# Router logits of eight batches by one product each, zero rows stored one block later, first queries and keys loaded ahead of the raw weights

## The reference

```python
xn = _layernorm(x)                                   # layer 0
s = attn0(xn)                                        # rms norm, queries, keys, values, running sums
router_logits = silu(xn @ router_w1) @ router_w2     # [8, 512, 16]
expert_probs = softmax(router_logits.transpose(0, 2, 1), axis=-1)   # over the 512 tokens
expert_weights, token_indices = top_k(expert_probs, 64)             # per sequence and expert
# gather these tokens, run the expert on them, add the weighted rows onto zeros
g = silu(output); x = x + s * g
xn = _layernorm(x)                                   # layer 1
s = attn1(layernorm(xn) * ln_scale + ln_bias) + ...  # 16 heads, softmax(q k / 16) v
g = silu(ffn1(xn))                                   # 8 experts, 2 per token, and one shared expert
x = x + s * g
```

## Time and profile before

| | us |
|---|---|
| median of 3 runs | 1772.76 (1771.67 to 1774.93) |
| the profiled execution, its own time | 1770.29 |
| its span, first to last instruction | 1768.3 |
| PE busy | 1576.7 (89%) |
| DVE busy | 1166.1 (66%) |
| ACT busy | 918.9 (52%) |
| POOL busy | 739.4 (42%) |
| granted TensorE clock over the span | 0.942 of full |

### The profile page before, as it was taken

One profiled execution on the slowest core, in us unless ns is written; L12 is line 12 of the kernel. 1 busy time (PEld: TensorE's weight loads), 2 busy tenths in 40 slices (PEclk: granted clock), 3 DMA queues, 4 the chain that ended last, 5 costly groups with the idle time before them and its releaser, 6 DMA issues.

```text
span 1768.3 us, 27041 instructions
## 1 busy us (share of the span) xinstructions
PE 1576.7 (89%) x9562; PEld 1140.3 (64%) x9562; DVE 1166.1 (66%) x1847; ACT 918.9 (52%) x1426; POOL 739.4 (42%) x664
## 2 busy tenths in 40 slices
PE   6679999999999549954999999999999999999976
PEld 4357767877877435632677777777777777777631
DVE  6747567567557156656766666777777777777647
ACT  2335545545545123311555556777776777676644
POOL 3406335334433255502323223556565555555410
PEclk9899999999999869975999999999999999999975
DMA  6715546445333268845233335767676667666464
GB/s 223 232 37 114 149 96 141 122 99 141 74 90 87 24 214 293 308 161 150 87 107 114 100 124 137 196 159 195 165 188 161 182 165 185 175 176 184 115 187 147
DMA packets 218918, 265.38 MB, mean 150 GB/s; under 512 B 19616, under 2 KB 160416, under 8 KB 218784
## 3 DMA queue, kind: packets, MB, share of 16 engines
q1 hardware_dynamic: 191904, 227.92, 42.6%
q0 software_dynamic: 26880, 35.73, 11.3%
HBM read 174.30 MB, written 88.75 MB: 149 GB/s over the span
## 4 chain that ended last, share of the span: by engine, by line
PE 39%; SPq 4%; DVE 3%; DMA 2%; ACT 1%; issue 1%; POOL 0%; DVEq 0%; ACTq 0%
PE a_hidden_bank L93 16%; PE a_bank L93 8%; PE a_bank L1522 5%; PE a_max_bank L1491 5%; PE a_score_bank L1512 3%; DMA a_ka<-qk 2%; SPq L1314 2%; SPq L1318 2%; PE a_max_bank L1537 1%; PE a_bank L1529 1%; DVE a_w20lo L1828 1%; ACT a_xThi L1670 1%; DVE a_neg_max L1787 1%; DVE a_hT1lo L1818 0%; SPq L1380 0%
## 5 line engine op out<-in xcount | busy, mean ns | idle before, releaser
L1648 ACT ACTIVATE a_prob<-a_score_bank 128x1024 f32<-128x1024 f32 x240 | 246.2, 1026 | 257.1 <-PE a_score_bank L1512 214.9
L1787 DVE TENSOR_REDUCE a_neg_max<-a_max_bank 128x2 f32<-128x1024 f32 x249 | 304.1, 1221 | 91.8 <-PE a_max_bank L1491 86.2
L1444 POOL DMA_INDIRECT fs<-a_y,a_token x80 | 127.1, 1589 | 189.2 <-ACT a_y L1696 164.9
L1491 PE MATMUL a_max_bank<-a_ka,a_qa 48*128 48x512 f32 x498 | 128.0, 511 | 23.4 <-DVE a_neg_max L1787 12.0
L1522 PE MATMUL a_bank<-a_prob,a_va 128*32 128x512 f32 x1024 | 147.2, 650 | 0.5 <-DVE a_ml L1796 0.5
L602 POOL DMA_INDIRECT f<-e_ye,c_slot_row x64 | 100.7, 1573 | 84.6 <-issue 64.6
L1810 DVE SCALAR_TENSOR_TENSOR a_tg<-a_tg,a_hidden_bank 128x512 f32<-128x512 f32 x112 | 76.7, 685 | 82.1 <-ACT a_tg L1658 82.1
L1512 PE MATMUL a_score_bank<-a_qa,a_ka 50*128 50x512 f32 x480 | 100.2, 413 | 5.1 <-DMA a_qa<-a_ml 2.7
L702 DVE TENSOR_TENSOR e_h<-e_bank,e_sge 128x512 f32<-128x512 f32 x64 | 44.3, 691 | 89.2 <-ACT e_sge L508 82.6
L358 PE MATMUL e_bank<-m_wqkv,x_rows 128*128 128x512 f32 (+1 forms) x256 | 91.3, 501 | 8.8 <-DVE e_qkv L642 8.8
L1491 PEld LDWEIGHTS a_max_bank<-a_ka,a_qa 48*128 48x128 f32 x498 | 47.9, 189 | 69.9 <-DVE a_neg_max L1787 23.3
(11 more groups left out here) (352 smaller groups left out, 4782.0 us busy)
## 6 DMA issues: line engine op xcount, KB each, us to landing
a_raw<-in_W SPq DMA_DIRECT2D x120, 512.0 KB
e_raw<-in_w SPq DMA_DIRECT2D x48, 512.0 KB, 3.8
a_qa<-qk SPq DMA_DIRECT2D x192, 64.0 KB
a_ka<-qk SPq DMA_DIRECT2D x192, 64.0 KB
xs<-c_pad SPq DMA_DIRECT2D x20, 516.0 KB
a_xg<-xs SPq DMA_DIRECT2D x20, 516.0 KB, 4.7
qk<-p_hi SPq DMA_DIRECT2D x32, 256.0 KB, 5.8
qk<-p_lo SPq DMA_DIRECT2D x32, 256.0 KB, 5.4
```

Source lines behind the costliest of these rows:

```text
L1444: nc.gpsimd.indirect_dma_start(f_rows, bass.IndirectOffsetOnAxis(token[x % 4][:, t:t + 1], 0), y[:, t, :], None, compute_op=ALU.add).then_ ...
L1491: nc.tensor.matmul(max_bank(g, m)[:, s, :], qa[q][rows, p, t * P:(t + 1) * P], ka[q][rows, p, :], start=True, stop=True).then_inc(p1_ps, 1)
L1648: nc.scalar.activation(prob[j % 2][:, 2 * p:2 * p + 2, :], score_bank(g, u)[:], ACT.Exp, scale=float(D) ** -0.5).then_inc(p_done, 1)
L1787: nc.vector.tensor_reduce(neg_max[:, g % 2, :, T * p + t], max_bank(g, m)[:], AX.X, ALU.max, negate=True).then_inc(mx_done, 1)
```

## The change

- `layer0_norm`, SP: `x[2]` and `x[3]` are loaded behind `rw2`, and later ones four turns ahead instead of two. `wqkv` and `wout` are loaded after the store of turn 3. The eight stores of zeros leave this block. The load of `rw2` waits for POOL's new fill.
- `layer0_norm`, PE, ACT and DVE: `rw2` lies in the middle of a tile of 240 columns of zeros. For turn n a window of 128 columns is taken, such that the 16 experts come to stand at rows 16n to 16n+15 of one PSUM bank, and the eight turns are accumulated in it: one product of 128 by 512 a turn in place of four of 128 by 16. ACT copies the bank once at the end; DVE's eight copies go. The result has (sequence, expert) on the partitions already.
- `layer0_norm`, POOL: fills the tile with zeros, and the six instructions for `m.r2`, `m.r2sq` and `m.r2neg` run in each turn over 4 columns, between one turn's `rstd` and the next.
- `layer0_mix_and_experts`: PE's four transposes of the logits are gone; the maximum and the exponential read `k.logits` in SBUF. SP stores the eight tiles of zeros behind the loads of the first expert's weights.
- `layer1_attend_and_feed`: SP issues `load_qk(0)` ahead of the two `load_w`; ACT does `high_x(0)` ahead of the two `high_w`.

```diff
@@ layer0_norm, SP
             sp.dma_start(rw1[:], w["rw1"]).then_inc(r_in, 16)
-            sp.dma_start(rw2[:], w["rw2"]).then_inc(r_in, 16)
-            sp.dma_start(m.wqkv[:], w["wqkv"]).then_inc(m.w_in, 16)
+            sp.wait_ge(half_set, 2)
+            sp.dma_start(rw2[:, P - E0:P], w["rw2"]).then_inc(r_in, 16)
+            load_x(2)
+            load_x(3)
             for n in range(NB):
-                if n + 2 < NB:
-                    load_x(n + 2)
+                if n + 4 < NB:
+                    load_x(n + 4)
                 sp.wait_ge(xn_done, n + 1)
                 sp.dma_start(at(xn_b, n), xn[n % 2][:]).then_inc(xn_out[n % 2], 16)
-            sp.dma_start(m.wout[:], w["wout"]).then_inc(m.w_in, 16)
-            for c in range(NB):
-                sp.dma_start(at(f_b, c), k.pad[:, :, 0:D]).then_inc(m.zeroed, 16)
+                if n == 3:
+                    sp.dma_start(m.wqkv[:], w["wqkv"]).then_inc(m.w_in, 16)
+                    sp.dma_start(m.wout[:], w["wout"]).then_inc(m.w_in, 16)
@@ PE
-                if n >= 2:
-                    pe.wait_ge(lg_sb, n - 1)
-                for t in range(T):
-                    ins = nc.tensor.matmul(B[6 + n % 2][:, t * E0:(t + 1) * E0], hT[:, n % 2, t * P:(t + 1) * P], rw2[:], start=True, stop=True)
-                ins.then_inc(lg_ps, 1)
+                first = (NB - 1 - n) * E0
+                nc.tensor.matmul(B[6][:], rw2[:, first:first + P], hT[:, n % 2, :], start=n == 0, stop=n == NB - 1).then_inc(lg_ps, 1)
@@ ACT, behind its loop
+            act.wait_ge(lg_ps, NB)
+            nc.scalar.activation(k.logits[:], B[6][:], ACT.Copy).then_inc(lg_sb, 1)
+            act.wait_ge(lg_sb, 1)
@@ POOL
+            first.step(nc.gpsimd.memset(m.half[:], -0.5))
+            first.step(nc.gpsimd.memset(rw2[:], 0.0))
             for n in range(NB):
+                now = slice(n * T, (n + 1) * T)
                 pool.wait_ge(veps_done, n + 1)
                 nc.gpsimd.tensor_tensor(rstd[:, n, :], veps[:, n, :], m.half[:, 0:T], ALU.pow).then_inc(rstd_done, 1)
-            pool.wait_ge(rstd_done, NB)
-            ... (six instructions over all 32 columns)
+                pool.wait_ge(rstd_done, n + 1)
+                own.step(nc.gpsimd.tensor_tensor(small[:, 0, now], flat_rstd[:, now], flat_rstd[:, now], ALU.mult))
+                own.wait()
+                ... (the same six instructions over the turn's 4 columns)
+                own.step(nc.gpsimd.tensor_tensor(m.r2[:, now], small[:, 2, now], m.half[:, now], ALU.pow))
@@ DVE
-                if n >= 3:
-                    logits(n - 3)
-            for n in range(NB - 3, NB):
-                logits(n)
-            dve.wait_ge(lg_sb, NB)
@@ layer0_mix_and_experts, SP
                 load(i, 0)
+            for c in range(NB):
+                sp.dma_start(at(f_b, c), k.pad[:, :, 0:D]).then_inc(m.zeroed, 16)
@@ PE
-            for t in range(T):
-                ins = nc.tensor.transpose(GATE[:, t * P:(t + 1) * P], k.logits[:, t].rearrange("p b e -> p (b e)"), k.ident[:])
-            ins.then_inc(choice_ps, 1)
@@ ACT and DVE
-            nc.scalar.activation(ex, GATE[:], ACT.Exp, bias=neg_max[:], accum_out=total[:]).then_inc(choice_exp, 1)
+            nc.scalar.activation(ex, k.logits[:], ACT.Exp, bias=neg_max[:], accum_out=total[:]).then_inc(choice_exp, 1)
-            dve.wait_ge(choice_ps, 1)
-            nc.vector.tensor_reduce(neg_max[:], GATE[:], AX.X, ALU.max, negate=True).then_inc(choice_done, 1)
+            nc.vector.tensor_reduce(neg_max[:], k.logits[:], AX.X, ALU.max, negate=True).then_inc(choice_done, 1)
@@ layer1_attend_and_feed, SP
             load_x(0)
+            load_qk(0)
             load_w(0, 0)
             load_w(1, 0)
-            load_qk(0)
             load_qk(1)
@@ ACT
+            high_x(0)
             high_w(0, 0)
             high_w(1, 0)
-            high_x(0)
```

53 lines of the change are left out of this document (24 added, 29 removed).

## The result

The change made the kernel faster, by more than forecast: 1760.72 us median (1758.33 to 1762.83, 4 runs) beside 1772.22 (1771.08 to 1774.93, 4 runs) of the kernel before on the same chip. The ratio is 0.9933, with a 95% interval of 0.9915 to 0.995. I had forecast 1766.4, with a range of 1763.0 to 1772.0: the gain is 11.5 us, not 6.4. The profiled execution of after took 1758.33 us, with a span of 1756.6.

What follows compares the result with a forecast made beforehand. A chain of waits, not engine load, was taken to bound the two changed stretches, and PE the rest. Gains of 1.6 + 0.4 + 4.4 = 6.4 us take the median from 1772.8 to 1766.4 us, range 1763.0 to 1772.0.

Steps and rivals of the forecast that it cites:

- Norm block, 1.6 forecast: layer0_norm: earlier loads and the new logits path end the block at 49.9 instead of 51.48, 1.6 us gained.
- POOL for the pacemaker: layer0_norm: with the factors in every turn, POOL takes 4.0 us a turn, longer than PE and ACT's 3.65, and sets the pace.
- the ring: layer0_norm: PE and ACT's cycle of hidden, silu and copies, 3.65 us a turn; alone it puts the last hidden at 45.1.
- rival of a contended power: layer0_norm: DVE's work slows POOL's powers, 4.4 us a turn, 2.8 us lost; total 1769.2 us, chance 0.12.
- rival of a far slower POOL: layer0_norm: semaphore hand-overs beside DVE make POOL's turn 5.5 us, costing 10.5; total 1776.9 us, chance 0.10.
- Experts' start, 0.4 forecast: Start of the experts' block: without the transposes the exponential waits only for its table load, 0.4 us gained, bounds 0 and 0.7.
- Attention block, 4.4 forecast: Start of the attention block: keys and low_x both come earlier, so DVE's first maximum does, 4.4 us gained (2.7 to 4.4).
- the landing: Attention block's start: turn 0's keys land 4.01 us after their issue ends, as in the loop, at 812.3.
- rival of early keys: Attention block's start: keys land before 811.9, low_x is last, 1 to 1.6 us more gained; 1765.1 us, chance 0.10.
- the loop: Last block's loop: PE's own work sets its pace, so its length stays unchanged and the 4.4 us gained ahead remain.
- late keys: Attention block's start: keys land as late after their issue as before (5.7 us), 1.7 less gained; 1768.1 us, chance 0.10.
- eaten gain: Shifted blocks: PE's clock steps down elsewhere or late weights catch the loop, two to five us given back; 1771 us, chance 0.12.

Runs made afterwards that it cites:

- e2: The changed kernel, unchanged, run and traced a second time: 1760.40 us, ratio 0.9934 to the kernel before.
- e7: The changed kernel with POOL's six factor instructions behind its loop again, over all 32 columns at once: 1762.65 us, ratio 0.9952 to before.
- e11: The kernel before with only the new load order of x, wqkv and wout in layer0_norm: 1768.40 us, ratio 0.9985 to before.
- e12: The changed kernel with only layer0_norm's load order of x, wqkv and wout put back: 1762.48 us, ratio 0.9956 to before.
- e8: The changed kernel with the eight stores of zeros back at the end of the norm block: 1761.81 us, ratio 0.9946 to before.
- e3: The kernel before with only the two reorderings (SP's and ACT's) at the attention block's start: 1767.56 us, ratio 0.9973 to before.
- e1: The kernel before, unchanged, run and traced a second time: 1769.63 us, 2.9 less than the runs beside it, ratio 0.9989.
- e5: The kernel before with only SP's reordering at the attention block's start, ACT's order as before: 1771.27 us, ratio 1.0 to before.
- e10: The kernel before with ten extra unread 128 x 512 products in PE's gaps in the choice of tokens: 1767.42 us, ratio 0.9988 to before.
- e13: The kernel before with ten unread products of 128 x 16 at the very start of PE's list: 1768.44 us, ratio 0.9986 to before.
- e18: The kernel before with ten unread products of 128 x 16 at the start of layer1_route: 1770.02 us, ratio 1.0003 to before.
- e9: The changed kernel with ten extra unread 128 x 512 products in PE's gaps in the choice of tokens: 1759.22 us, ratio 0.9942 to before.
- e14: The changed kernel with 31 unread products of 128 x 16 at the start of PE's list: 1765.58 us, ratio 0.9974 to before.

## Why the prediction was right or wrong

**Norm block, 1.6 forecast.** 0.87 and 1.90 in the two traces of after, 1.4 on the mean. The load order does what I put; the mechanism I set on top is wrong. I held POOL for the pacemaker at 4.0 us a turn. Its turn is 3.9 and its eighth `rstd` ends at 38.45, near my 38.9. But DVE's waits for POOL (4.7 us) end inside PE's slack: `hidden` starts every 3.65 us without a break, from 23.86 to 45.75 in after, and from 22.83 to 44.72 in e2. The block's end hangs on when that ring starts. e7 takes the chain away and the block ends where it did. That I had 45.1 for the last `hidden` by POOL and by the ring alike was luck of two numbers that met. The rival of a contended power fell: 1.04 us on the mean of the eight (8.3 us in all), though DVE worked beside it. The Trainium skill's sentence on shared interfaces (GPSIMD Engine Reference, Specifications) is not shown by the power in this run. One small add of the chain (L217) took 0.25 us in the first turn and 0.40 on the mean of eight; what slows it is not shown. The rival of a far slower POOL fell with the 3.9; a turn has seven instructions, not the eight that I wrote there.

**Product, copy, zeros.** The new product takes 1.02 us, as put (1.0); it gains nothing in this block (e11, e12). The zeros cost this block nothing in either place (e8), as put.

**Experts' start, 0.4 forecast.** The exponential starts 1.71 after the block's start before (53.19 - 51.48) and 1.30 now (51.91 - 50.61): 0.41.

**Attention block, 4.4 forecast.** With the piece at its place, as in the trace that I read, the two edits give nearly that: 10.83 in e3, where I had written 10.9. But there two errors cancel: the keys' issue ended 7.1 us after the block's start, where I had 6.0, and they landed 2.8 later, where I had 4.0. In the kernel after the piece is elsewhere, and it is 9.67: 5.56 gained against the trace of before, and only some 2 against e1, which has no piece either. The step that failed here is the landing: "in the loop, where the chain passes through the same transfer, 4.01", and "With only `xg` ahead I take the latter". It was 2.76. The rival of early keys, with `low_x` last, was the better one: `low_x` and the keys meet at 809.65 and 809.68. The estimate from the Trainium skill, 2.15 us for 64 KB (DMA: Bandwidth & Descriptors, Anatomy of one DMA), lies 0.6 below what the trace shows, nearer than the 4.01 of a loop in which other transfers run. The Trainium skill gives that fit for DMAs that GpSimd issues, and these are issued by SP.

**The sum up to the loop came out, the rest did not.** At the loop's start I had 6.4 us; the traces have 6.97 and 6.26 for after and e2. That is in part luck: the 6.26 are 1.90 of the norm block and 5.40 from the attention block's start to the loop, less 1.04 that the stretch between lost, and that stretch alone moves by 6 us among the traces. The term that failed is the loop, which I had put at nothing: "The loop is PE's, so the 4.4 stay" and "the loop's length unchanged". From the loop's start to the end it took 934.0 us in the trace of before and 929.3 in that of after, 4.7 less, which is what the traced pair gained beyond the 7.0 at the loop's start. But the length lies between 929.3 and 935.8 in the twenty traces of the table, and no kernel stands out. The trace of before is one of the long ones, that of after is the shortest. On the mean the ten kernels with both attention edits have 931.4, the other ten 933.0, or 932.6 without e5, the longest. So the 4.7 us of the first pair are for the most part the luck of two executions. The first quarter of the loop doesn't tell them apart: the 65th of ACT's 256 records of `a_prob` begins 237.8 to 239.2 us after the loop's start in all twenty, 238.2 in before and 238.6 in after. The differences come later, and no run here shows why.

**One execution as the base.** The whole sum was built on one trace whose attention block started slowly (15.23, where the same program also took 11.73) and whose loop was long.

**What stays open.** Medians do not rest on one execution, and they say 11.5 and 12.1 for the whole, or 10 if after's 1760.5 is set against the 1770.6 of the kernel before over all groups and e1. The stages explain 1.4 (norm), 0.4 (experts), 4.0 for the attention block as a mean over executions with and without the piece (13.5 over before, e1, e10, e11, e13 and e18, against 9.5 over the six kernels with the change's attention start, new logits and no idle products in front), and perhaps 1.2 in the loop: 7.0. In runs without a profile I can't see which group an execution of before belongs to; were it always that of 15.2 us, the attention block's term would be 5.8 and the sum 8.8. Between one and five microseconds have no place. In the pair with filled gaps (e9, e10) nothing need be left over: their 8.2 lie between 7.0 and 8.8. So the rest may hang on where PE's clock falls to half in the choice of tokens; the traces do not bear that out, as their means there are no shorter with the change (52.8 against 52.2). That it hangs on where PE's instructions lie is suggested by e14, which lost 5.2 us with 31 idle products of which the trace accounts for 1 to 2; e13's 2.8 are no more than e1 shows for an unchanged kernel. Both are argued, not shown, and the cause of this part stays open.

**Chances.** I gave 0.66 to faster, and faster it is. The rivals of late keys, of a contended or far slower POOL and of an eaten gain all fell; early keys, at 0.10, was the nearest. The range's lower end (1763.0) is my own range's 1764.5 less some 1.4 us for early keys, and has nothing for the spread of the one execution on which the sum was built.

## What to carry to other kernels

Before a stall in a trace is priced, look for a second execution of the same kernel: here one stretch took 15.2 or 11.7 us with the same code, and a sum built on the one carries that into the forecast. Time the unchanged kernel against itself as well: its two medians differed by 2.9 us here, so a difference of that size decides nothing alone. When two conditions end at about the same time, both have to move, or the edit is worth nothing; and a chain of small instructions on a slow engine costs nothing while it starts early enough, even if its turn is longer than that of the ring which it feeds. Idle work added to an engine to test a placement must be measured itself: an fp32 product stands in the trace twice (31 as x62, 50 as x100), and at the start of a list or in front of a wait such products are not free.

## What the runs showed of the hardware

- A 16 KB fetch of instructions (0.9 to 1.8 us on its queue) that falls on the start of a block full of loads goes with a landing of a 512 KB load some 1.1 to 1.9 us later (5.1 to 5.5 against 3.9 to 4.0, or 6.3 against 4.4 to 5.0 with small slices behind it), and with 0.5 to 1.6 us more for what SP issues then. That the fetch is the cause is argued from twenty traces, not shown: no run moved it at will. In the same program it fell at 803.2 in one execution and at 781.8 in another.
- PE's granted clock in the choice of tokens, where it waits much, goes with the length of that stretch: 53.6 to 53.9 us at a mean of 0.81, 50.0 with the gaps filled and a mean of 0.93. The same program took 51.2 and 53.8.
- The same kernel differs from one execution to the next by up to 12.5 us (before, as e1: 1764.4 to 1776.9). The kernel after stayed within 4.5 us in nine runs (1758.3 to 1762.8), but its near variants did not (e9: 1755.6 to 1765.4).
- A 64 KB slice lands 2.8 us after the end of the issue of its row of six when, of large loads, only 512 KB are ahead, 3.8 where 1.5 MB are ahead (e1), and 5.7 where 1.5 MB and a piece are ahead.
